# Rank-32 products of the experts as one rounded pass over three stacked copies

## What is computed

```python
# layer 0: top 2 of 8 experts; 2 x 160 slots of tokens per expert (one block of 160 for each choice)
h = gelu(einsum('ecd,edf->ecf', buf, w1) + b1)             # 256 -> 1024
y = einsum('ecf,efd->ecd', h, w2) + b2                     # 1024 -> 256
y = y + einsum('ecr,erd->ecd', gelu(einsum('ecd,edr->ecr', buf, wd)), wu)   # 256 -> 32 -> 256
out = out + y[e, slot] * keep * top_p
sh = gelu(xt @ sw1 + sb1) @ sw2 + sb2 + gelu(xt @ swd) @ swu                 # shared expert
out = out + 0.2 * sh
# layer 1
out = x @ (weight * scale_weight[:, None]).T + bias
```

## Time and profile before

| | |
|---|---|
| median of the runs | 971.4 us |
| profiled execution | 964.8 us, of it span 963.0 us |
| mean granted TensorE clock | 0.98 |
| busy PE (matmul) | 908.6 us, 94% of the span |
| busy PEld (weight load) | 742.3 us |
| busy DVE, ACT, POOL | 577.6, 437.6, 435.0 us |

### The profile page before, as it was taken

The page is one execution under the profiler, slowest core; times in us unless marked ns, Lnnn a source line. Parts: engine busy times, 40 slices in busy tenths (PEclk is TensorE's granted clock), DMA queues, the critical chain, the costliest instruction groups (busy, mean ns, idle before and its releaser), DMA issues.

```text
span 963.0 us, 15641 instructions
## 1 busy us (share of the span) xinstructions
PE 908.6 (94%) x5536; PEld 742.3 (77%) x5536; DVE 577.6 (60%) x1189; ACT 437.6 (45%) x880; POOL 435.0 (45%) x290
## 2 busy tenths in 40 slices
PE   5999999999999999999999978799999979989998
PEld 4888888888688788888888766668888857856677
DVE  6889889898830333454364735477667574336632
ACT  3667666676520434545342372352352434246620
POOL 5667667675237343355551111029816244115610
PEclk9999999999999999999999988899999989979999
DMA  7110100100052543544022040001111010000001
GB/s 299 34 33 16 33 24 25 33 17 16 1 224 82 205 141 123 166 144 123 14 76 70 11 176 0 1 23 55 44 35 42 6 50 1 1 1 2 3 1 44
DMA packets 20766, 57.61 MB, mean 60 GB/s; under 512 B 2896, under 2 KB 12016, under 8 KB 17648
## 3 DMA queue, kind: packets, MB, share of 16 engines
q1 hardware_dynamic: 19184, 52.79, 16.3%
q0 software_dynamic: 1536, 4.20, 1.4%
HBM read 48.59 MB, written 8.39 MB: 59 GB/s over the span
## 4 chain that ended last, share of the span: by engine, by line
PE 86%; DVE 8%; ACT 3%; issue 2%; POOL 1%; POOLq 0%; DVEq 0%; ACTq 0%
PE banks L100 22%; PE banks L101 21%; PE banks L102 21%; PE banks L876 6%; PE banks L1178 3%; PE banks L1206 3%; PE banks L1165 2%; PE banks L921 2%; DVE stats L1242 1%; PE banks L988 1%; DVE banks L1651 1%; PE banks L888 1%; DVE xn L1253 1%; DVE x L1237 1%; PE banks L828 1%
## 5 line engine op out<-in xcount | busy, mean ns | idle before, releaser
L1816 ACT ACTIVATE banks<-banks,small 128x512 f32<-128x512 f32 x128 | 84.9, 663 | 79.7 <-DVE small L1302 79.7
L102 PE MATMUL banks<-arenaC_rounded,arenaD_rounded 128*128 128x512 f32 (+2 forms) x272 | 94.5, 347 | 0.0
L100 PE MATMUL banks<-xnT_rounded,arenaD_rounded 128*128 128x512 f32 (+1 forms) x228 | 91.0, 399 | 2.9 <-POOL arenaC_rounded L647 1.5
L1302 DVE TENSOR_REDUCE small<-banks 128x1 f32<-128x512 f32 x128 | 86.9, 679 | 10.5 <-PE banks L102 10.5
L101 PE MATMUL banks<-s_tok_rounded,arenaD_rounded 128*128 128x512 f32 (+1 forms) x228 | 91.1, 400 | 0.0
L102 PE MATMUL banks<-xnT_rounded,arenaC_rounded 128*128 128x512 f32 x192 | 76.5, 399 | 0.0
L102 PE MATMUL banks<-xnT_rounded,arenaD_rounded 128*128 128x512 f32 x192 | 75.8, 395 | 0.0
L100 PE MATMUL banks<-arenaC_rounded 128*128 128x512 f32 (+1 forms) x192 | 71.1, 370 | 1.2 <-DVE arenaC_rounded L1427 1.2
L1317 DVE SCALAR_TENSOR_TENSOR arenaC<-banks,small,arenaC 128x512 f32<-128x512 f32 x96 | 71.2, 742 | 0.0
L101 PE MATMUL banks<-arenaD_rounded,arenaC_rounded 128*128 128x512 f32 (+1 forms) x192 | 68.5, 357 | 0.0
L676 POOL TENSOR_TENSOR arenaD_rounded<-arenaD,arenaB_rounded 128x1024 fp32r<-128x1024 f32 (+1 forms) x12 | 37.3, 3128 | 52.2 <-ACT arenaB_rounded L1864 52.2
(11 more groups left out here) (375 smaller groups left out, 2555.8 us busy)
## 6 DMA issues: line engine op xcount, KB each, us to landing
arenaD<-in_wexp SPq DMA_DIRECT2D x8, 1060.0 KB, 5.4
arenaD<-in_wexp SPq DMA_DIRECT2D x8, 1024.0 KB, 5.0
arenaC<-in_wqkv SPq DMA_DIRECT2D x16, 384.0 KB, 3.1
arenaD<-in_wexp SPq DMA_DIRECT2D x8, 512.0 KB, 3.5
slots<-arenaB SPq DMA_DIRECT2D x1, 2560.0 KB, 10.6
arenaB<-in_sw SPq DMA_DIRECT2D x1, 2084.0 KB, 7.4
arenaC<-in_wo SPq DMA_DIRECT2D x1, 2048.0 KB, 15.1
arenaC<-slots SPq DMA_DIRECT2D x8, 256.0 KB, 2.7
```

The lines of the kernel that those rows point to most:

```text
L100: pe.matmul(o, r(lhs[0]), r(rhs[0]), start=start, stop=False)
L102: return pe.matmul(o, r(lhs[1]), r(rhs[0]), start=False, stop=stop)
L1302: dve.tensor_reduce(negmax[:, n % 4:n % 4 + 1], bank[3 + n % 4][:, :], AX.X, ALU.max, negate=True).then_inc(max_done, 1)
L1816: act.activation(prob[r], prob[r], ACT.Exp, bias=negmax[:, r:r + 1], accum_out=rowsum[:, r:r + 1]).then_inc(exp_done, 1)
```

## The change

The rank-32 product is written as one rounded matmul over all 128 rows of the array. `wu` is laid out on the host in three copies, at rows 0 to 31, 32 to 63 and 64 to 95, with zeros below (`_copies`), so its load is 128 KB instead of 32. ACT rounds it (`round_up`, a tenth piece in `w_rounded`), and DVE writes the rest into rows 64 to 127 of the rounded matrix (`up_rest`), so that these rows are hi, hi, rest, zero. The down matrix is repeated four times (`four`, `wd4`), so that the rank tile comes out of TensorE in four copies over 128 partitions; its GELU stays in PSUM, DVE copies it rounded to `aE` and subtracts at rows 32 to 63: hi, rest, hi, hi. One matmul then adds hi x hi, rest x hi and hi x rest. `up_rest` stands in DVE's `expert` behind the subtraction of n = 3, and in `shared_split` at f = 3 of half 0. `h_rounded` and `h_split` now count nine an expert, and TensorE's fifth hidden tile waits for a split too. The repeated down matrices lie in memory that the token rows hold until they are scattered; so in the first expert ACT waits for the scatter before it rounds the down matrix, POOL's down piece goes last, and TensorE waits for it before the first `turn`.

In the shared expert `shared_rows` no longer waits at its start for all GELUs; it waits for the rank tile's split at its first rank-32 product. The bias of the linear layer is rounded over all partitions with its rest at rows 32 to 63, and `two_rows`, ones in rows 0 and 32 and zeros elsewhere, picks both up in one matmul; `row_sum`, made in DVE's prologue, and one more ACT activation in `fold(7)` make it.

```diff
-        wu = [w[0:RANK, WPACK:WPACK + D] for w in wexp]
+        wu = [w[:, WPACK:WPACK + D] for w in wexp]
+        wu_hi = [part(arenaB, 7936, D), part(arenaB, 15944, D)]
+        wd4_hi, wd4 = ([part(xn_flat, 1024 + 512 * q + at, 4 * DC * RANK, r="p (c k r) -> p c k r", c=DC, k=4) for q in range(2)]
+                       for at in (0, 256))
-        aE = arenaC[0:RANK, 3840:3840 + SLOTS]
+        aE = part(arenaC, 3840, SLOTS)
+        def four(v):
+            return v.unsqueeze(2).to_broadcast([P, DC, 4, RANK])
...
+        two_rows = part(arenaC, 5440, P)
+        row_sum = part(small, 1524, 1)
...
-            def split_expert(e, w, hi, wd_hi_):
+            def split_expert(e, q, w, hi, late=False):
+
+                def down(n):
+                    pool.wait_ge(w_rounded, 10 * e + n)
+                    pool.tensor_tensor(r(wd4[q]), four(wd_of(w)), rounded(wd4_hi[q]), ALU.subtract).then_inc(w_split, 1)
...
+                part_of(4, w[:, 0:W_D], hi[:, 0:W_D])
+                if not late:
+                    down(5)
+                part_of(6 if late else 7, w[:, W_2:W_2 + 1024], hi[:, -2048:-1024])
+                part_of(8 if late else 9, w[:, W_2 + 1024:WPACK], hi[:, -1024:])
+                if late:
+                    down(9)
...
-                    if n == HID_BANKS:
-                        pe.wait_ge(hid_done, HID0 + 9 * e + 1)
-                    if n > HID_BANKS:
-                        pe.wait_ge(h_split, NF * e + n - HID_BANKS)
+                    if n >= HID_BANKS:
+                        pe.wait_ge(h_split, 9 * e + n - HID_BANKS + 1)
...
-                        mm = product(pe, bank[2 + n % HID_BANKS][0:P if n else RANK, 0:SLOTS], w,
+                        mm = product(pe, bank[2 + n % HID_BANKS][:, 0:SLOTS], w,
...
-                            pe.wait_ge(h_split, NF * e + f + 1)
+                            pe.wait_ge(h_split, 9 * e + f + 2)
...
-                    mm = pe.matmul(o, aE[:, s * P:s * P + rows], wu[q], start=False, stop=True)
+                    mm = pe.matmul(o, r(aE[:, s * P:s * P + rows]), r(wu_hi[q]), start=False, stop=True)
...
+            pe.wait_ge(w_split, 4)
             turn(0, 0, 0)
...
+                if n - 4 == NF:
+                    pe.wait_ge(hS_split, NF + 1)
...
             def shared_rows(b):
-                pe.wait_ge(shid_done, (NF + 1) * (b + 1))
...
-                    pe.matmul(o, aS[:, t * P:(t + 1) * P], swu, start=False, stop=True).then_inc(sh_ready, 1)
+                    if t % ST == 0:
+                        pe.wait_ge(hS_split, (NF + 1) * (b + 1))
+                    pe.matmul(o, r(aS[:, t * P:(t + 1) * P]), r(swu_hi), start=False, stop=True).then_inc(sh_ready, 1)
...
-                    one = ones_r[0:1, :].bitcast(F32R)
-                    pe.matmul(o, one, r(lin_bias_hi[0:1, :]), start=False, stop=False)
-                    pe.matmul(o, one, r(lin_bias[0:1, :]), start=False, stop=True).then_inc(g_ready, 1)
+                    pe.matmul(o, r(two_rows), r(lin_bias_hi), start=False, stop=True).then_inc(g_ready, 1)
...
+            dve.tensor_tensor(row_sum, ident[:, 0:1], ident[:, RANK:RANK + 1], ALU.add)
...
+            def up_rest(e, u, u_hi):
+
+                dve.wait_ge(w_rounded, 10 * e + 10)
+                dve.tensor_tensor(r(u_hi[64:P, :]), u[64:P, :], rounded(u_hi[64:P, :]), ALU.subtract)
+
             def expert(e, q, pair, last=False):
-                for f in range(NF + 1):
-
-                    if f < NF:
-                        dve.wait_ge(hid_done, HID0 + 9 * e + f + 2)
-                        dve.tensor_copy(r(hE_hi[:, f, :]), bank[2 + (f + 1) % HID_BANKS][:, 0:SLOTS]).then_inc(h_rounded, 1)
-                    if f:
-                        dve.wait_ge(h_rounded, NF * e + f)
-                        dve.tensor_tensor(r(hE[:, f - 1, :]), bank[2 + f % HID_BANKS][:, 0:SLOTS], rounded(hE_hi[:, f - 1, :]),
-                                          ALU.subtract).then_inc(h_split, 1)
+                for n in range(NF + 2):
+
+                    if n <= NF:
+                        dve.wait_ge(hid_done, HID0 + 9 * e + n + 1)
+                        dve.tensor_copy(r(hE_hi[:, n - 1, :] if n else aE), bank[2 + n % HID_BANKS][:, 0:SLOTS]).then_inc(h_rounded, 1)
+                    if n:
+                        f = n - 2
+                        v = bank[2 + (n - 1) % HID_BANKS][:, 0:SLOTS]
+                        o, v, h = (hE[:, f, :], v, hE_hi[:, f, :]) if n > 1 else (aE[RANK:2 * RANK, :], v[RANK:2 * RANK, :], aE[RANK:2 * RANK, :])
+                        dve.wait_ge(h_rounded, 9 * e + n)
+                        dve.tensor_tensor(r(o), v, rounded(h), ALU.subtract).then_inc(h_split, 1)
+                    if n == 3:
+                        up_rest(e, wu[q], wu_hi[q])
...
             def shared_split(b, tiles):
                 for f in tiles:
+                    dve.wait_ge(shid_done, (NF + 1) * b + f + 1)
+                    if b == 0 and f == 3:
+                        up_rest(NE, swu, swu_hi)
+                    v = bank[((NF + 1) * b + NF) % 4]
...
+                    else:
+                        dve.tensor_copy(r(aS[:, b * S:(b + 1) * S]), v[:, :]).then_inc(hS_rounded, 1)
...
+                    if f == NF:
+                        a = aS[RANK:2 * RANK, b * S:(b + 1) * S]
+                        dve.wait_ge(hS_rounded, (NF + 1) * (b + 1))
+                        dve.tensor_tensor(r(a), v[RANK:2 * RANK, :], rounded(a), ALU.subtract).then_inc(hS_split, 1)
...
-                    v, h = w[:, W_D:W_B], wd_hi_
+                    v, h = four(wd_of(w)), wd_hi_
...
+            def round_up(u, u_hi):
+
+                act.copy(r(u_hi), u).then_inc(w_rounded, 1)
...
-                        act.activation(aE, bank[2][0:RANK, 0:SLOTS], ACT.Gelu).then_inc(hid_done, 1)
+                        act.activation(v, v, ACT.Gelu).then_inc(hid_done, 1)
...
-            for n in range(9):
-                round_weights(wexp[0], wexp_hi[0], wd_flat[0], n)
+            for n in (0, 1, 2, 3, 5, 6, 7, 8):
+                round_weights(wexp[0], wexp_hi[0], wd4_hi[0], n)
+            act.wait_ge(slots_put, 16 * 2 * NT)
+            round_weights(wexp[0], wexp_hi[0], wd4_hi[0], 4)
...
+                    act.activation(r(two_rows), ones[:, :], ACT.Copy, scale=row_sum)
                     ins = act.copy(r(lin_bias_hi), lin_bias)
...
+def _copies(u):
+
+    return np.concatenate([u, u, u, np.zeros((P - 3 * RANK, u.shape[1]), u.dtype)], 0)
```

More of the change, by code:

```diff
@@ L202, in build @@
         w2_hi = [w[:, DC * FF:4096].rearrange("p (f d) -> p f d", f=NF) for w in wexp_hi]
-        wd_hi = [part(small, 820 + DC * RANK * q, DC * RANK, r="p (c r) -> p c r", c=DC) for q in range(2)]
         hE_hi = part(arenaB, 4096, NF * SLOTS, r="p (f n) -> p f n", f=NF)
@@ L669, in _, with part_of @@
                                             oob_is_err=False).then_inc(slots_put, 16)
-            def split_expert(e, w, hi, wd_hi_):
-                for n, (v, h) in ((4, (w[:, 0:W_D], hi[:, 0:W_D])), (5, (w[:, W_D:W_B], wd_hi_)),
-                                  (7, (w[:, W_2:W_2 + 1024], hi[:, -2048:-1024])), (9, (w[:, W_2 + 1024:WPACK], hi[:, -1024:]))):
-                    pool.wait_ge(w_rounded, 9 * e + n)
-                    pool.tensor_tensor(r(v), v, rounded(h), ALU.subtract).then_inc(w_split, 1)
-            wd_flat = [v.rearrange("p c r -> p (c r)") for v in wd_hi]
-            split_expert(0, wexp[0], wexp_hi[0], wd_flat[0])
+            def split_expert(e, q, w, hi, late=False):
+                def down(n):
+                    pool.wait_ge(w_rounded, 10 * e + n)
+                    pool.tensor_tensor(r(wd4[q]), four(wd_of(w)), rounded(wd4_hi[q]), ALU.subtract).then_inc(w_split, 1)
+                def part_of(n, v, h):
+                    pool.wait_ge(w_rounded, 10 * e + n)
+                    pool.tensor_tensor(r(v), v, rounded(h), ALU.subtract).then_inc(w_split, 1)
+                part_of(4, w[:, 0:W_D], hi[:, 0:W_D])
[5 more added lines that the diff above has]
+                    down(9)
+            split_expert(0, 0, wexp[0], wexp_hi[0], late=True)
             with pool.Fori(0, NE // 2 - 1) as pair:
-                split_expert(2 * pair + 1, wexp[1], wexp_hi[1], wd_flat[1])
-                split_expert(2 * pair + 2, wexp[0], wexp_hi[0], wd_flat[0])
-            split_expert(NE - 1, wexp[1], wexp_hi[1], wd_flat[1])
-            split_expert(NE, sw, sw_hi, sw_hi[:, W_D:W_B])
+                split_expert(2 * pair + 1, 1, wexp[1], wexp_hi[1])
+                split_expert(2 * pair + 2, 0, wexp[0], wexp_hi[0])
+            split_expert(NE - 1, 1, wexp[1], wexp_hi[1])
+            split_expert(NE, 0, sw, sw_hi)
             for q in range(2):
@@ L952, in shared_hidden @@
                     pe.wait_ge(shid_done, n - 3)
+                if n - 4 == NF:
+                    pe.wait_ge(hS_split, NF + 1)
                 for c in range(DC):
```

(15 more changed lines are left out.)

25 lines of the change are left out of this document (14 added, 11 removed).

## The result

| | before | changed |
|---|---|---|
| median of the runs | 971.4 us | 1000.4 us (997.7 to 1001.9) |
| ratio, 95% interval | | 1.0325 (1.0293 to 1.0357) |
| profiled execution, span | 964.8, 963.0 us | 1001.9, 1000.1 us |
| mean granted clock | 0.98 | 0.95 |

The change costs 29 us. The prediction said 1005.0, within 979 to 1013. The profiled execution of before was quicker than the median of its runs, that of the changed kernel slower, so the two spans lie 37 us apart.

A forecast was written before the change was run, and what follows sets the result against it. TensorE was taken to bound the kernel, 86% of the chain that ended last. Span 963.0 - 23.6 (TensorE's savings) + 36.4 (block) + 20.8 (clock) = 996.6 us; on the median 1005.0, range 979 to 1013.

The forecast's parts named there:

- The block: Routed experts: DVE's `up_rest` stands still until POOL's 2048-column subtraction ends; TensorE waits 4.55 us an expert, 36.4 us for eight.
- The clock: Routed experts: TensorE's idle of some 4.4 us halves its clock behind it; 2.6 us lost each, 20.8 for eight.
- The rival in which the clock holds: Routed experts: `up_rest` is blocked but the clock stays up; 984.2 us, up to 994; chance 0.20.
- The gain of TensorE: Routed experts: rank-32 products become ordinary rounded products; 1.92 us saved an expert, 15.4 us for eight.
- move with it: Routed experts: ACT's longer first GELU makes all behind it 0.09 us late; TensorE's five waits on split tiles shift too.
- Shared expert and linear layer: Shared expert saves 5.6 us on eight rank-32 products and 0.7 on a dropped wait; linear layer's bias products save 1.9.
- The sum: Whole kernel: 996.6 us of span; adding the median's difference from the profiled execution gives 1005.0 us.
- no block: Routed experts: POOL and DVE don't meet, `up_rest` costs 2.5 us for eight; median 950.3 us; chance 0.12.
- In every overlap of two such instructions: Trace of before: whenever DVE and POOL instructions with SBUF inputs overlap, it agrees with an exclusive lock held by the first.

The follow-up runs named there:

- fill: Changed kernel with 28 rounded matmuls, output thrown away, on TensorE ahead of the tile that waits for DVE; 981.7 us, ratio 1.013.
- early: Changed kernel with `up_rest` one tile earlier, behind the subtraction of n = 2 instead of n = 3; 947.9 us, ratio 0.981.
- late_pool: Changed kernel with POOL's 2048-column subtraction held back until ACT has rounded one piece more, from the second expert's weights on; 948.5 us, ratio 0.979.
- narrow: Changed kernel with the 64x256 subtraction of `up_rest` cut to 64x16 at the same place; 992.4 us, ratio 1.027.
- block_before: Kernel before plus only one 64x256 DVE subtraction, both inputs in SBUF, behind each routed expert's third tile subtraction; 1018.3 us, ratio 1.054.
- no_rest: Changed kernel without the eight `up_rest` subtractions in the routed experts; 948.0 us, ratio 0.979.

## Why the prediction was right

**The block.** Said: `up_rest` at 4.6 us, ending 0.3 us behind POOL, TensorE idle 4.4. Measured: 4.39, 0.27, 4.23. In time: the stage is 184.7 us with the block and the clock kept (`fill`), of which 1.5 us is a half clock at its start, and 147.0 without it; 36.2 us against the predicted 36.4. `early` and `late_pool` show the order to decide, `narrow` that size doesn't, `block_before` that nothing else is needed. `up_rest` came 0.42 us behind POOL rather than 0.23, and the shorter block comes from that: it starts 0.51 us behind the third subtraction, where the sum has 0.41, and that subtraction starts 0.09 us ahead of POOL instead of 0.18. Why, no run shows.

**The clock.** Said: 2.6 us an expert, 20.8. Measured by `fill`: 18.9. The range it was given, 0 to 27, was needed: each of the eight stops has a half-clock stretch that begins in it or at most 0.4 us behind it, but these lasted from 3.4 to 10.2 us. That their mean came so near the one stretch of 5.2 us from which the term was taken is in part luck. The rival in which the clock holds is out.

**The gain of TensorE.** Said: 15.4 us in the experts. Measured in `no_rest`: 161.0 - 147.0 = 14 (160.9 by the same marks, 13.9). The product itself is exact to the reading: the rows of an expert went from 10.86 to 8.95 us, 1.91 against the predicted 1.92. The missing 1.5 us is in the hidden tiles, where an expert's nine went from 8.13 us to 8.26 in most experts and from 8.87 to 9.14 in the two with the longer wait: the splits come 0.1 to 0.3 us later, which I had named ("move with it") and then not entered in the sum. That term was mis-sized.

**Shared expert and linear layer.** Said: 6.3 and 1.9. From 58.9 us before to 52.4 in `early` is 6.5, and 58.8 with the part undone. The changed kernel's own profile has 54.4: two thirds of the gain. Of the 2.0 us that are missing, three stops without a shown releaser are 1.3. The stretch with the linear layer went from 68.2 us to 66.5, 1.7.

**The sum.** Said: 996.6 us of span; measured 1000.1. The 3.5 us are: 1.0 ahead of the experts (where a half-clock stretch from 258.9 us on is, which the profile of before hasn't), 0.9 in the experts (whose first 3.4 us run at half clock, which was not in the sum), 1.8 in the shared one, less 0.2 behind. On the medians it was 29.0 us instead of 33.6, and the step that was off is the last one: I carried the 6.6 us by which the median of before lies above its profiled execution over to the changed kernel. They are no fixed amount. Before's profile was a quick execution; on the other chips its runs went from 964.5 us to 973.0, at granted clocks of 0.98 to 0.97. The changed kernel's profile lies 1.5 us above its own median.

**The rival "no block".** Its time, 950.3 us, is that of every kernel of this study that has the change and not the full block, to within 3 us.

**What it said too widely.** "In every overlap of two such instructions" is more than the trace of before holds. Here DVE's sum of 512 columns, both inputs in SBUF, starts while POOL raises two columns to a power, both inputs in SBUF, and is not held; it takes its plain 0.69 us:

```profile
531.91 1.03 POOL L563 TENSOR_TENSOR rstd<-veps,mhalf 128x2 f32<-128x2 f32 x1 [21.73 <-DVE veps L1248]
...
532.38 0.69 DVE L1237 TENSOR_TENSOR x<-x,arenaC 128x512 f32<-128x512 f32 x1
```

Nor were DVE's subtractions with two inputs in SBUF held beside POOL's gathers (512 columns in the shared expert of before: 0.68 to 0.69 us for all sixteen, beside a gather or not). What was shown to hold them are POOL's subtractions and like arithmetic over 512 columns or more; where the line runs isn't shown.

## What to carry to other kernels

Before a DVE instruction with both inputs in SBUF, or a DVE copy from SBUF to SBUF, is put into a queue on which TensorE waits, look which POOL instruction runs then: if a long POOL subtraction on SBUF began first, the price is the rest of that instruction, whatever the size of one's own. Put it where POOL idles, a few tenths of a microsecond ahead of POOL, take one operand from PSUM, or cut POOL's instruction up. And price a stop of TensorE of some 4 us half as high again, for the clock (18.9 us on 36.2 here).

## What was not expected of the hardware

A DVE copy of 64x256 from SBUF to SBUF is held by POOL just as a subtraction with two SBUF inputs is (4.27 us against 4.39). And TensorE, at steps of 0.12 us, stopped in the shared expert for 0.2 to 0.9 us at a time, with nothing in the profile that released it, in 5 of 11 profiles. That it ran short of instructions is my guess. POOL's gathers ran in the same stretch, but so they did in `early`, which has no stop; the cause wasn't tried, and stays open.
